# State-space layer of a decoder: residual sum moved from VectorE and GpSimd to TensorE and ScalarE

## The chip, the core and the metric

The kernel runs on one core of one Trainium2 chip. The metric is the device time of one execution in microseconds. The engines are TensorE (PE, with its weight loads as PEld), VectorE (DVE), ScalarE (ACT), GpSimd (POOL) and SyncE (SP, which issues the DMAs). Each engine takes its own instructions in the order in which the program lists them. They meet only at semaphores: an instruction waits until a counter has reached a value, and a finished instruction raises a counter.

## The reference, cut to what matters

The network is a decoder of two layers over x of 64 sequences, 128 tokens and 128 channels, all in float32. The fourth of its six steps is the state-space layer:

```python
x = _layernorm(x + _L1_attn_ref(x, W_in, b_in, conv_w, conv_b, x_proj_w, dt_proj_w,
                                dt_bias, A_log, D_param, W_out, b_out))
# in _L1_attn_ref, E = 256 channels, N = 16 states:
z = x @ W_in + b_in
xc, xr = z[..., :E], silu(z[..., E:])
xc = silu(causal_conv(xc, 4 taps) + conv_b)
dt, Bm, Cm = split(xc @ x_proj_w)
delta = softplus(dt @ dt_proj_w + dt_bias)
h_t = exp(delta * A) * h_(t-1) + delta * xc * B_t      # 16 states per channel
y_t = sum over states of h_t * C_t
return ((y + xc * D_param) * xr) @ W_out + b_out
```

The x that goes in is itself the layer norm of the sum before it. So the layer has to form: normalised x, plus the output product, plus the output bias.

## The kernel before, in words

The layer is `phase_scan`. It handles the 64 sequences in 16 groups of four, so a tile holds 128 partitions by 512 columns (by 1024 where both halves of the 256 channels are in one tile). Every group g has a body on each engine, and every body loops over the 16 states n. What an engine does at a state is written out by hand, so the order of the work is the order of these loops and nothing else. Work for the groups g+1, g+2 and g+3 and the leftovers of group g-1 are slotted between the states.

A state goes round the engines in this way.

- POOL multiplies `du` by B (`drive_state`, line 1872) into one of three `drive` buffers.
- ACT computes the decay, one instruction for each half (`decay_state`, line 2025). There is one `decay` tile in PSUM, so each half waits until DVE has scanned the same half of the state before.
- DVE runs two scans, one for each half (`scan_state`, line 2239), and then, for 13 of the 16 states, multiplies the state by C (`read_state`, line 2252). For the states 3, 7 and 13 ("aside") POOL does that product (line 1882).
- PE adds the product to `y_ps` with the identity as stationary operand (`sum_state`, line 2387; `sum_aside`, line 2395).

Around these, PE also makes 156 "lots" for the next phase (`make_lot`, line 2314, into one of the two banks `f0_ps` and `f1_ps`). ACT copies each lot out (`take_lot`, line 2066) and SP stores it.

These are the places that the change touches:

- `normalise` on ACT (line 1932), in the slot of state 13 for group g+3: it writes normalised x of a group into the tile `xs`, with four instructions.
- `turn` on PE (line 2324), at state 0 for group g+2: it transposes `xs`. ACT copies the result to `xT` at state 2 (`copy_xT`, line 1943).
- `add_bo` on POOL (line 1819), at state 3 for group g+2 and twice ahead of the loop: x = `xs` + output bias.
- `gate_y` on DVE (line 2261), after state 0, for group g-1: it ends that group's y and raises `y_ready`.
- `project_out` on PE (line 2410), at state 1 and after `sum_state(1)` and the lot of that slot, for group g-1: eight products of 128 by 128 into the bank `f1_ps`; then it raises `o_ready`.
- `leave_group` on DVE (line 2268), after state 3, for group g-1: x = `f1_ps` + x; then it raises `x_steps`.

After the loop, group 15 goes through `gate_y`, `project_out` and `leave_group` once more, with nothing beside them. Ahead of the loop stands a prologue in which DVE adds the residual of the phase before to x (`combine`, line 2167) and finds the statistics. The root of the last batch of statistics on ACT (line 1922) stands ahead of the first decay.

In ACT's body the slot of state 2 is this, and the decay of state 3 comes behind it:

```python
for n in range(states):
    decay_state(g, s, n)
    for unit in taken_at(g, n, n + 1):
        take_lot(unit)
    ...
    if n == 2 and ahead(g, 2):
        copy_xT(g + 2, s)
```

Of the kernel before, what the change touches and what calls it, by code (L numbers as in the profile page):

```python
# [10 lines left out]
ALU = mybir.AluOpType  # L11
# [1507 lines left out]
def phase_scan(core):  # L1519
# [24 lines left out]
    with ExitStack() as ctx:  # L1544
# [15 lines left out]
        early = sb("s_early", [128, halves, taps - 1])  # L1560
        skip_w = sb("s_skip_w", [128, halves, 128])
        shift = sb("s_shift", [128, B])
        xs = sb("s_xs", [128, GB, 128])
        xT = sb("s_xT", [128, GB, taps - 1 + T])
        conv = sb("s_conv", [128, halves, GB, T])
        conv_sig = sb("s_conv_sig", [128, halves, GT])
# [41 lines left out]
        rates = sig("s_rates")  # L1608
        prepared = sig("s_prepared", 6)
        x_normed = sig("s_x_normed")  # L1610
        bo_added = sig("s_bo_added")
        x_turned = sig("s_x_turned")
        xT_ready = sig("s_xT_ready")
        z_ready = sig("s_z_ready", 4)
# [187 lines left out]
        def _(pool):  # L1802
# [11 lines left out]
            nc.gpsimd.memset(xT[:, :, 0:taps - 1], 0.0).then_inc(cleared.sem, 1)  # L1814
            nc.gpsimd.memset(dtT[:, :], 1.0).then_inc(cleared.sem, 1)

            def add_bo(g, s):
                pool.wait_ge(x_normed.sem, x_normed.at(g, 1))
                nc.gpsimd.tensor_tensor(x[:, ds(g * GB, GB), :], xs[:, :, :],
                                        core.w["s_bo"][:, :].unsqueeze(1).broadcast_to([128, GB, 128]),  # L1820
                                        ALU.add).then_inc(bo_added.sem, 1)

            def fix_conv(g, s):

                pool.wait_ge(z_copied.sem, z_copied.at(g, halves))
# [61 lines left out]
            def body(g, s):  # L1887
                for n in range(states):
                    drive_state(g, s, n)
                    if n - 2 in aside:  # L1890
                        read_aside(g, n - 2)
                    if n == 1 and ahead(g, 1):
                        gate_u(g + 1, 1 - s)
                    if n == 3 and ahead(g, 2):
                        add_bo(g + 2, s)
                    if n == 7 and ahead(g, 1):
                        gate_res(g + 1, 1 - s)
                    if n == 12 and ahead(g, 1):
                        make_delta(g + 1, 1 - s)
                    if n == 13 and ahead(g, 1):  # L1900
                        mult_du(g + 1, 1 - s)
                    if n == 14 and ahead(g, 2):
                        fix_conv(g + 2, s)

            add_bo(0, 0)
            fix_conv(0, 0)
            gate_u(0, 0)
            add_bo(1, 1)
            gate_res(0, 0)
            make_delta(0, 0)  # L1910
            mult_du(0, 0)
# [4 lines left out]
        def _(act):  # L1916
# [7 lines left out]
            def normalise(g, s):  # L1924
                for n, batch in enumerate(batches):
                    if g in batch:
                        act.wait_ge(folded.sem, folded.at(n, 9))
                if behind(g, 1):
                    act.wait_ge(bo_added.sem, bo_added.at(g - 1, 1))
                    act.wait_ge(x_turned.sem, x_turned.at(g - 1, 1))  # L1930
                for j in range(GB):
                    last = nc.scalar.activation(xs[:, j, :], x[:, g * GB + j, :], ACT.Identity,
                                                bias=shift[:, ds(g * GB + j, 1)],
                                                scale=core.rstd[:, ds(g * GB + j, 1)])
                last.then_inc(x_normed.sem, 1)
# [93 lines left out]
            def body(g, s):  # L2029
# [4 lines that stand above are left out]
                    if n == 5 and ahead(g, 1):  # L2034
                        tanh_res(g + 1, 1 - s)
                        open_res(g + 1, 1 - s)
                    if n == 2 and ahead(g, 2):
                        copy_xT(g + 2, s)
                    if n == 4 and ahead(g, 1):
                        copy_proj(g + 1, 1 - s)  # L2040
                    if n == 6 and ahead(g, 1):
                        take_raw(g + 1, 1 - s)
                    if n == 8 and ahead(g, 1):
                        soft_exp(g + 1, 1 - s)
                    if n == 10 and ahead(g, 1):
                        soft_ln(g + 1, 1 - s)
                    if n == 11 and ahead(g, 2):
                        copy_conv(g + 2, s, 0)
                    if n == 12 and ahead(g, 2):
                        copy_conv(g + 2, s, 1)  # L2050
                    if n == 13 and ahead(g, 3):
                        normalise(g + 3, 1 - s)
                    if n == 14 and ahead(g, 2):
                        copy_res(g + 2, s, 0)
                        copy_res(g + 2, s, 1)
                    if n == 15 and ahead(g, 2):
                        tanh_conv(g + 2, s)
                        open_conv(g + 2, s)

            def take_lot(unit):  # L2060
                j, n = unit // parts, unit % parts
# [68 lines left out]
            around(act, body)  # L2130
            for unit in taken_at(NG, 0, states):
                take_lot(unit)

        @block.vector
        def _(dve):
# [125 lines left out]
                nc.vector.tensor_tensor(res_gate[:, s, :, :], y_ps[:, :, :], res_gate[:, s, :, :],  # L2261
                                        ALU.mult).then_inc(y_ready.sem, 1)

            def leave_group(g, s):
                dve.wait_ge(o_ready.sem, o_ready.at(g, 1))
                dve.wait_ge(bo_added.sem, bo_added.at(g, 1))
                here = x[:, ds(g * GB, GB), :].rearrange("p b d -> p (b d)")
                nc.vector.tensor_tensor(here, f1_ps, here, ALU.add).then_inc(x_steps.sem, 1)

            def body(g, s):  # L2270
                for n in range(states):
                    scan_state(g, s, n)
                    if n not in aside:
                        read_state(g, s, n)
                    if n == 0 and behind(g, 1):
                        gate_y(g - 1, 1 - s)
                    if n == 3 and behind(g, 1):
                        leave_group(g - 1, 1 - s)

            around(dve, body)  # L2280
            gate_y(NG - 1, 1)
            leave_group(NG - 1, 1)

        @block.tensor
        def _(pe):
# [32 lines left out]
            def turn(g, s):  # L2318
# [2 lines left out]
                if behind(g, 1):  # L2321
                    pe.wait_ge(z_copied.sem, z_copied.at(g - 1, 3))
                for j in range(GB):
                    last = nc.tensor.transpose(f0_ps[:, j * 128:(j + 1) * 128], xs[:, j, :], core.ident[:, :])
                last.then_inc(x_turned.sem, 1)

            def project_conv(g, s, m):
# [69 lines left out]
                last.then_inc(aside_summed.sem, 1)  # L2397

            def project_out(g, s):
                pe.wait_ge(y_ready.sem, y_ready.at(g, 1))  # L2400
                if ahead(g, 2):
                    pe.wait_ge(z_copied.sem, z_copied.at(g + 2, 4))
                elif ahead(g, 1):
                    pe.wait_ge(raw_taken.sem, raw_taken.at(g + 1, 2))
                else:
                    pe.wait_ge(x_steps.sem, x_steps.at(g - 1, 1))
                lot_gone(g + 1, 1, 1)
                for j in range(GB):
                    for m in range(halves):
                        last = nc.tensor.matmul(f1_ps[:, j * 128:(j + 1) * 128], res_gate[:, s, m, j * 128:(j + 1) * 128],  # L2410
                                                core.w["s_w_out"][:, m, :], start=(m == 0), stop=(m == halves - 1))
                last.then_inc(o_ready.sem, 1)

            def body(g, s):
# [1096 lines left out]
```

## Time and profile before

| what | us |
| --- | --- |
| median of 3 runs | 2777.88 (2777.25 to 2780.86) |
| the profiled execution's own time | 2776.81 |
| its span, first to last instruction | 2774.9 |
| first scan of the state-space layer | 1095.9 |
| last `leave_group` of the layer | 2045.5 |

The profile is that of one execution. Between its span and its own time lie 1.9 us. In the timelines a row is: start, length, engine, line of the kernel, operation, written tile <- read tiles, shape, and how many instructions of the same kind were merged; in square brackets stands how long the engine was idle just before, and what ended that.
### The profile page before, as it was taken

The page shows a single profiled execution, that of the slowest core. Times are in us where ns is not written, and L with a number is a line of the kernel's source. Part 1 is how long each engine was busy: PE and PEld are TensorE (multiplying, and loading weights), DVE is VectorE, ACT ScalarE, POOL GpSimd, SP SyncE. Part 2 cuts the span into 40 slices and gives each one's busy share as a digit, 9 for nine tenths or more (in the row PEclk, how much of TensorE's full clock was granted, in tenths as well). Part 3 has the DMA queues.
Part 4 walks back from the last instruction along what each step waited for, and adds up shares of the span by engine and source line. Part 5 has one row for each costly group of instructions (what it writes and reads, how often), then busy time and mean ns, then how long its engine had stood idle before and what let it go on. Part 6 is the DMA issues. An engine that isn't in the chain of part 4 may idle for free. (4 is left out here: it accounts for less than half of the span.)

```text
span 2774.9 us, 42509 instructions
## 1 busy us (share of the span) xinstructions
PE 2466.6 (89%) x13058; PEld 1468.1 (53%) x13058; DVE 2235.6 (81%) x3698; ACT 1722.6 (62%) x3447; POOL 2000.4 (72%) x1817
## 2 busy tenths in 40 slices
PE   7969999989979976989898899898989999999675
PEld 5646666656646652333333333343348888877232
DVE  5879999856634449999999999999867777777898
ACT  7847777743312226667766776766655665554897
POOL 5539999847746664999999999999836666666244
PEclk9979999999989988999999999999999999999556
DMA  5921111001135535445454554544633323332000
GB/s 164 422 76 22 24 23 22 10 27 44 41 109 162 155 111 192 175 185 188 176 199 161 198 184 171 193 176 176 218 123 84 87 86 87 88 87 74 12 24 28
DMA packets 238434, 331.94 MB, mean 120 GB/s; under 512 B 46433, under 2 KB 186998, under 8 KB 217346
## 3 DMA queue, kind: packets, MB, share of 16 engines
q1 hardware_dynamic: 227538, 311.48, 33.8%
q0 software_dynamic: 9088, 16.94, 1.7%
q8 instruction: 109, 1.79, 0.3%
q14 instruction: 115, 0.94, 0.1%
q10 hardware_dynamic: 1584, 0.79, 0.1%
HBM read 231.45 MB, written 99.50 MB: 119 GB/s over the span
## 5 line engine op out<-in xcount | busy, mean ns | idle before, releaser
L1872 POOL TENSOR_TENSOR s_drive<-s_du,s_b_sb 128x1024 f32<-128x1024 f32 x256 | 600.3, 2359 | 40.1 <-DVE s_state_ps L2239 39.9
L2239 DVE TENSOR_TENSOR_SCAN s_state_ps<-s_decay_ps,s_drive 128x512 f32<-128x512 f32 x416 | 487.1, 1216 | 44.3 <-ACT s_decay_ps L2025 35.4
L2387 PE MATMUL s_y_ps<-s_read,w_ident 128*128 128x512 f32 x832 | 407.3, 616 | 89.0 <-DVE s_read L2252 88.8
L2025 ACT ACTIVATE s_decay_ps<-s_delta,neg_rate 128x508 f32<-128x508 f32 x512 | 340.8, 682 | 151.1 <-DVE s_state_ps L2239 93.4
L2387 PEld LDWEIGHTS s_y_ps<-s_read,w_ident 128*128 128x128 f32 x832 | 149.8, 192 | 323.0 <-DVE s_read L2252 182.9
L2252 DVE TENSOR_TENSOR s_read<-s_state_ps,s_c_sb 128x1024 f32<-128x1024 f32 x208 | 254.6, 1224 | 7.2
L1418 POOL DMA_INDIRECT m_y_scratch<-e_y,e_index x156 | 152.6, 978 | 91.1 <-DVE e_y L1464 49.3
L2686 POOL TENSOR_TENSOR c_share<-c_p,c_norm 128x1232 f32<-128x1232 f32 x64 | 148.2, 2315 | 83.0 <-DVE c_norm L2821 83.0
L743 ACT ACTIVATE b_pT<-b_turn_ps 77x512 f32<-77x512 f32 x256 | 144.3, 591 | 74.6 <-PE b_turn_ps L875 74.6
L2922 PE MATMUL c_f_ps<-c_ctxT,w_c_wqk 128*128 128x308 f32 x512 | 179.4, 438 | 6.2 <-DMA c_ctxT<-in_ctxT_dram 3.6
L1046 POOL DMA_INDIRECT m_rows_scratch<-m_xs,m_index x128 | 128.3, 1003 | 60.1 <-issue 39.9
L677 POOL TENSOR_TENSOR b_p<-b_p,b_top 128x1232 f32<-128x1232 f32 x64 | 143.9, 2248 | 35.8 <-DVE b_top L805 35.8
L2314 PE MATMUL s_f_ps<-w_c_wvo,s_lotT 128*128 128x512 f32 (+1 forms) x312 | 154.0, 600 | 14.2 <-ACT s_res L1959 10.3
L2066 ACT ACTIVATE s_stage<-s_f_ps 128x512 f32<-128x512 f32 (+1 forms) x156 | 89.9, 588 | 118.0 <-PE s_f_ps L2314 111.4
L2965 PEld LDWEIGHTS c_turn_ps<-c_vp,c_pT 128*128 128x128 f32 (+1 forms) x1280 | 152.4, 192 | 14.1 <-issue 6.2
L2735 ACT ACTIVATE c_k<-c_f_ps,key_bias 128x308 f32<-128x308 f32 x256 | 132.6, 518 | 43.1 <-PE c_f_ps L2922 42.4
L2965 PE MATMUL c_turn_ps<-c_vp,c_pT 128*128 128x128 f32 (+1 forms) x1280 | 153.7, 275 | 4.6 <-ACT c_pT L2760 4.6
L875 PE MATMUL b_turn_ps<-w_ident,b_p 128*77 128x128 f32 x1024 | 152.6, 282 | 0.0
L2755 ACT ACTIVATE c_pT<-c_turn_ps 128x512 f32<-128x512 f32 x128 | 69.7, 595 | 131.9 <-PE c_turn_ps L2956 131.9
L2818 DVE TENSOR_REDUCE c_norm<-c_p 128x16 f32<-128x1232 f32 x64 | 91.9, 1436 | 69.8 <-ACT c_p L2747 69.8
L683 POOL TENSOR_TENSOR b_p<-b_p,b_norm 128x1232 f32<-128x1232 f32 x64 | 143.9, 2249 | 2.2 <-DVE b_norm L811 2.2
L2940 PE MATMUL c_s_ps<-c_k,c_xT 128*128 128x308 f32 x512 | 143.2, 421 | 0.7 <-DVE c_p L2809 0.7
(376 smaller groups left out, 6153.7 us busy)
## 6 DMA issues: line engine op xcount, KB each, us to landing
s_b_sb<-s_bc_scratch SPq DMA_DIRECT2D x64, 1024.0 KB, 6.2
s_c_sb<-s_bc_scratch SPq DMA_DIRECT2D x64, 1024.0 KB, 5.4
c_vp_scratch<-s_stage SPq DMA_DIRECT2D x152, 256.0 KB, 2.6
c_vp<-c_vp_scratch SPq DMA_DIRECT2D x64, 576.0 KB, 4.2
m_rows_scratch<-fill SPq DMA_DIRECT2D x33, 1040.0 KB, 27.0
e_w<-in_m_we_dram SPq DMA_DIRECT2D x39, 384.0 KB, 3.2
e_xg<-m_rows_scratch SPq DMA_DIRECT2D x39, 260.0 KB, 3.4
s_read<-m_y_scratch SPq DMA_DIRECT2D x32, 256.0 KB, 3.1
```

The costliest lines, as they stand in the source:

```text
L743: nc.scalar.activation(pT[:, j, :, :], turn_ps[0:S2, j % 2, :].rearrange("p (r t) -> p r t", t=128), ACT.Copy).then_inc(pT_ready.sem, 1)
L875: last = nc.tensor.transpose(turn_ps[0:S2, j % 2, r * 128:(r + 1) * 128], p[:, s, per * r + j, :], core.ident[:, :])
L1418: nc.gpsimd.indirect_dma_start(y_dram[:, :], bass.IndirectOffsetOnAxis(index[:, t % y_slots, j:j + 1], 0), y[:, t % y_slots, j, :], None, ...
L1872: nc.gpsimd.tensor_tensor(drive[:, (g * states + n) % drives, :, :], du[:, s, :, :], b_sb[:, n, :].unsqueeze(1).broadcast_to([128, halves, ...
L2025: nc.scalar.activation(decay[:, m, :, 1:], delta[:, s, m, :].rearrange("p (b t) -> p b t", t=T)[:, :, 1:], ACT.Exp, scale=core.neg_rate[:, ...
L2239: nc.vector.tensor_tensor_scan(home[:, h, :], decay[:, h, :, :].rearrange("p b t -> p (b t)"), drive[:, (g * states + n) % drives, h, :], ...
L2252: nc.vector.tensor_tensor(read[:, r % deep, :, :], state[:, :, :], c_sb[:, n // per_chunk % 2, n % per_chunk, :].unsqueeze(1).broadcast_to ...
L2314: nc.tensor.matmul(f_ps[0:lot_width(j), bank, :], lotT[:, j % lot_slots, 0:lot_width(j)], wvo[:, 4 * part:4 * part + 4, :].rearrange("p h ...
L2387: last = nc.tensor.matmul(y_ps[:, m, :], core.ident[:, :], read[:, r % deep, m, :], start=False, stop=False)
L2686: nc.gpsimd.tensor_tensor(share[:, i % 2, :].rearrange("p (s h) -> p h s", h=heads), p[:, i % p_slots, :, :], norm[:, i % 2, :].unsqueeze( ...
L2922: nc.tensor.matmul(f_ps[:, mine % 2, 0:GB * S2], core.w["c_wqk"][:, h, :], ctxT[:, g % 2, :], start=True, stop=True).then_inc(front_ready. ...
L2965: last = nc.tensor.matmul(y_ps, pT[0:width(c), i % 2, c, :], vp[0:width(c), i % vp_slots, c, :], start=(c == 0), stop=(c == lumps - 1))
```

## The change

- `xs` goes away. ACT's `normalise` writes normalised x over x, in place, and no longer waits for `add_bo` and `turn` of the group before. `turn` reads x.
- `add_bo` on POOL goes away.
- `project_out` on PE gets two products of 512 columns ahead of its eight: the identity times x of the group, and the identity times the bias, repeated for the four sequences. All ten accumulate in `f1_ps`. The wait for `y_ready` now stands behind these two.
- `leave_group` leaves DVE. ACT gets it as a copy of `f1_ps` to x, behind `copy_xT` in the slot of state 2, and behind its last lots for group 15.

```diff
-            def add_bo(g, s):
-                pool.wait_ge(x_normed.sem, x_normed.at(g, 1))
-                nc.gpsimd.tensor_tensor(x[:, ds(g * GB, GB), :], xs[:, :, :],
-                                        core.w["s_bo"][:, :].unsqueeze(1).broadcast_to([128, GB, 128]),
-                                        ALU.add).then_inc(bo_added.sem, 1)
...
-                    if n == 3 and ahead(g, 2):
-                        add_bo(g + 2, s)
...
-            add_bo(0, 0)
             fix_conv(0, 0)
             gate_u(0, 0)
-            add_bo(1, 1)
             gate_res(0, 0)
...
-                if behind(g, 1):
-                    act.wait_ge(bo_added.sem, bo_added.at(g - 1, 1))
-                    act.wait_ge(x_turned.sem, x_turned.at(g - 1, 1))
                 for j in range(GB):
-                    last = nc.scalar.activation(xs[:, j, :], x[:, g * GB + j, :], ACT.Identity,
+                    last = nc.scalar.activation(x[:, g * GB + j, :], x[:, g * GB + j, :], ACT.Identity,
...
                     if n == 2 and ahead(g, 2):
                         copy_xT(g + 2, s)
+                    if n == 2 and behind(g, 1):
+                        leave_group(g - 1)
...
+            def leave_group(g):
+                act.wait_ge(o_ready.sem, o_ready.at(g, 1))
+                nc.scalar.activation(x[:, g * GB:(g + 1) * GB, :].rearrange("p b d -> p (b d)"), f1_ps,
+                                     ACT.Copy).then_inc(x_steps.sem, 1)
...
             for unit in taken_at(NG, 0, states):
                 take_lot(unit)
+            leave_group(NG - 1)
...
-            def leave_group(g, s):
-                dve.wait_ge(o_ready.sem, o_ready.at(g, 1))
-                dve.wait_ge(bo_added.sem, bo_added.at(g, 1))
-                here = x[:, ds(g * GB, GB), :].rearrange("p b d -> p (b d)")
-                nc.vector.tensor_tensor(here, f1_ps, here, ALU.add).then_inc(x_steps.sem, 1)
...
-                    if n == 3 and behind(g, 1):
-                        leave_group(g - 1, 1 - s)
...
-                    last = nc.tensor.transpose(f0_ps[:, j * 128:(j + 1) * 128], xs[:, j, :], core.ident[:, :])
+                    last = nc.tensor.transpose(f0_ps[:, j * 128:(j + 1) * 128], x[:, g * GB + j, :], core.ident[:, :])
...
             def project_out(g, s):
-                pe.wait_ge(y_ready.sem, y_ready.at(g, 1))
...
                 lot_gone(g + 1, 1, 1)
+                pe.wait_ge(x_normed.sem, x_normed.at(g, 1))
+                nc.tensor.matmul(f1_ps, core.ident[:, :], x[:, g * GB:(g + 1) * GB, :].rearrange("p b d -> p (b d)"),
+                                 start=True, stop=False)
+                nc.tensor.matmul(f1_ps.rearrange("p (b d) -> p b d", b=GB), core.ident[:, :],
+                                 core.w["s_bo"][:, :].unsqueeze(1).broadcast_to([128, GB, 128]),
+                                 start=False, stop=False)
+                pe.wait_ge(y_ready.sem, y_ready.at(g, 1))
                 for j in range(GB):
                     for m in range(halves):
                         last = nc.tensor.matmul(f1_ps[:, j * 128:(j + 1) * 128], res_gate[:, s, m, j * 128:(j + 1) * 128],
-                                                core.w["s_w_out"][:, m, :], start=(m == 0), stop=(m == halves - 1))
+                                                core.w["s_w_out"][:, m, :], start=False,
+                                                stop=(j == GB - 1 and m == halves - 1))
                 last.then_inc(o_ready.sem, 1)
```

## Rows read from the trace of the kernel before

**Rows 1.** Windows: one group of the loop, scan to scan
```profile
core 0: us, PE busy (x) PEld busy (x) DVE busy (x) ACT busy (x) POOL busy (x), PEclk, DMA share, GB/s
1500.20:1558.90 58.70, 52.75 (x134) 22.32 (x132) 54.75 (x48) 41.00 (x62) 54.92 (x26) 1.00 0.48 180
```
**Rows 2.** Line 2239 (DVE's scans): its engine sat idle until (us, times)
```profile
  ACT s_decay_ps L2025: 48.6, 75
```
**Rows 3.** Timeline of DVE in that group
```profile
1514.87 1.22 DVE L2252 TENSOR_TENSOR s_read<-s_state_ps,s_c_sb 128x1024 f32<-128x1024 f32 x1
...
1519.70 2.33 DVE L2239 TENSOR_TENSOR_SCAN s_state_aside<-s_decay_ps,s_drive 128x512 f32<-128x512 f32 x2
1521.95 0.66 DVE L2268 TENSOR_TENSOR x<-s_f_ps,x 128x512 f32<-128x512 f32 x1
1522.53 2.33 DVE L2239 TENSOR_TENSOR_SCAN s_state_ps<-s_decay_ps,s_drive 128x512 f32<-128x512 f32 x2
...
1526.27 2.35 DVE L2239 TENSOR_TENSOR_SCAN s_state_ps<-s_decay_ps,s_drive 128x512 f32<-128x512 f32 x2 [0.15 <-ACT s_decay_ps L2025]
...
1540.47 2.35 DVE L2239 TENSOR_TENSOR_SCAN s_state_ps<-s_decay_ps,s_drive 128x512 f32<-128x512 f32 x2 [1.16 <-ACT s_decay_ps L2025]
```
**Rows 4.** Timeline of ACT in that group
```profile
1515.49 0.58 ACT L1943 ACTIVATE s_xT<-s_f_ps 128x512 f32<-128x512 f32 x1
1517.44 0.69 ACT L2025 ACTIVATE s_decay_ps<-s_delta,neg_rate 128x508 f32<-128x508 f32 x1 [1.38 <-DVE s_state_ps L2239]
...
1524.38 0.59 ACT L1992 ACTIVATE s_bc_rows<-s_f_ps 32x512 f32<-32x512 f32 x1 [1.62 <-PE s_f_ps L2355]
...
1538.22 0.60 ACT L2066 ACTIVATE s_stage<-s_f_ps 128x512 f32<-128x512 f32 x1 [1.69 <-PE s_f_ps L2314]
```
**Rows 5.** Timeline of PE and its weight loads in that group
```profile
1516.14 0.30 PEld L2387 LDWEIGHTS s_y_ps<-s_read,w_ident 128*128 128x128 f32 x2 [0.64 <-DVE s_read L2252]
...
1517.97 1.02 PE L2314 MATMUL s_f_ps<-w_c_wvo,s_lotT 128*128 128x512 f32 x2
1518.82 1.95 PE L2410 MATMUL s_f_ps<-w_s_w_out,s_res_gate 128*128 128x128 f32 x16
...
1526.18 1.98 PE L2387 MATMUL s_y_ps<-s_read,w_ident 128*128 128x512 f32 x4 [1.84 <-DVE s_read L2252]
```
**Rows 6.** Lines 2268 and 1819: lengths in ns (min/median/max), first and last start
```profile
L2268 DVE TENSOR_TENSOR x<-s_f_ps,x x16: 662/663/691, 1169.9 to 2045.5; 128x512 f32<-128x512 f32 x16
...
L1819 POOL TENSOR_TENSOR x<-s_xs,w_s_bo x16: 1279/1292/1735, 1044.9 to 1865.8; 128x512 f32<-128x512 f32 x16
```
**Rows 7.** Timeline of PE and DVE in group 14
```profile
1928.21 1.95 PE L2410 MATMUL s_f_ps<-w_s_w_out,s_res_gate 128*128 128x128 f32 x16
...
1929.95 2.33 DVE L2239 TENSOR_TENSOR_SCAN s_state_aside<-s_decay_ps,s_drive 128x512 f32<-128x512 f32 x2
...
1936.43 3.54 PE L2387 MATMUL s_y_ps<-s_read,w_ident 128*128 128x512 f32 x4 [2.51 <-DVE s_read L2252]
...
1944.66 2.34 DVE L2239 TENSOR_TENSOR_SCAN s_state_aside<-s_decay_ps,s_drive 128x512 f32<-128x512 f32 x2 [0.89 <-ACT s_decay_ps L2025]
```
**Rows 8.** Windows: the stretch of group 14 behind PE's pause
```profile
1936.40:1939.90 3.50, 3.47 (x5) 0.98 (x5) 3.40 (x3) 3.16 (x4) 3.50 (x3) 0.54 0.71 281
```
**Rows 9.** Timeline of PE and DVE in group 15 and at the layer's end
```profile
1992.42 1.95 PE L2410 MATMUL s_f_ps<-w_s_w_out,s_res_gate 128*128 128x128 f32 x16
...
1992.44 2.33 DVE L2239 TENSOR_TENSOR_SCAN s_state_aside<-s_decay_ps,s_drive 128x512 f32<-128x512 f32 x2
...
2043.44 2.02 PE L2410 MATMUL s_f_ps<-w_s_w_out,s_res_gate 128*128 128x128 f32 x16 [0.77 <-ACT s_stage L2066]
```
**Rows 10.** Timeline of the prologue, DVE and ACT
```profile
1057.08 1.47 DVE L2167 TENSOR_TENSOR x<-x,s_read 128x512 f32<-128x512 f32 x2
...
1059.37 4.36 DVE L2167 TENSOR_TENSOR x<-x,s_read 128x512 f32<-128x512 f32 x2
...
1093.56 0.25 ACT L1922 ACTIVATE stat_root<-rstd 128x52 f32<-128x52 f32 x1 [5.18 <-DVE rstd L2188]
```

More of the change, by code:

```diff
@@ L1562, in phase_scan @@
         shift = sb("s_shift", [128, B])
-        xs = sb("s_xs", [128, GB, 128])
         xT = sb("s_xT", [128, GB, taps - 1 + T])
@@ L1610, in phase_scan @@
         x_normed = sig("s_x_normed")
-        bo_added = sig("s_bo_added")
         x_turned = sig("s_x_turned")
@@ L2276, in body @@
                         gate_y(g - 1, 1 - s)
-                    if n == 3 and behind(g, 1):
-                        leave_group(g - 1, 1 - s)
             around(dve, body)
             gate_y(NG - 1, 1)
-            leave_group(NG - 1, 1)
         @block.tensor
```

## The prediction

> **What bounds the kernel now.** The change touches only the state-space layer, so I read that layer's rows and take the rest of the kernel as it is. The first view is a window over one group of its loop. In 58.70 us DVE is busy for 54.75, POOL for 54.92, PE for 52.75 and ACT for 41.00 [rows 1]. Three engines are nearly full, so the shares alone don't say which of them sets the pace. The second view does: what ended the idle time ahead of DVE's scans. In the whole layer it was ACT's decay, 75 times, 48.6 us in sum [rows 2], 3.0 us for each of 16 groups, and no other engine is named there. So DVE sets the pace, and where it pauses it waits for ACT. POOL and PE are full, but they follow.
>
> The third view is the timeline around the slot that changes. It shows how ACT, which is busy for only 41 of 58.7 us, comes to hold up DVE: at 1538.22 ACT starts the copy of a lot for which it had waited 1.69 us on PE, and DVE's scan at 1540.47 then starts 1.16 us late, because the decay stood behind that copy in ACT's queue [rows 3, 4]. A wait of ACT for PE is therefore a cost that reaches DVE. The change adds such a wait.
>
> **What is removed.** DVE's `leave_group` has 16 instructions of 663 ns [rows 6]. In the loop each costs DVE less than its length, since neighbours overlap a little: from its start at 1521.95 to the next scan at 1522.53 is 0.58 us [rows 3]. That is what one group gains on the engine that sets the pace. POOL's `add_bo` has 16 instructions of 1292 ns at the median [rows 6]; 14 are in the loop, where no scan was late through POOL [rows 2], so I take nothing for them. The two waits taken from `normalise` were for work of the group before, done more than a state's time ahead: nothing. `normalise` in place has the same four instructions, and `turn` the same four transposes.
>
> **What is added on PE.** Two products of 512 columns with the identity. The nearest row is a lot, one product of 512 columns: from 1517.97 to the next instruction at 1518.82 is 0.85 us [rows 5]. Two are 1.70 us for each group. From below I bound the pair by 0.85 us, if the repeated bias row should cost nothing; from above by 3.54 us, the length of two such products in the slowest row [rows 7]. I take 1.70, since these have the shape of the ordinary row. PE has room for that: 52.75 of 58.70 us. What counts is where they stand.
>
> **What is added on ACT, and the wait.** ACT's copy of `f1_ps` to x has the form of `copy_xT`, 0.58 us [rows 4]. Ahead of it ACT waits for `o_ready`. Behind it in ACT's queue stand the two decays of state 3, a lot, the decays of state 4 and the copies for `project_dt`; DVE waits for the decays, and POOL and PE wait for DVE. So I follow the chain in one ordinary group:
>
> - DVE's product of state 1 ends at 1514.87 + 1.22 = 1516.09 [rows 3]; PE, which waited for it, starts `sum_state(1)` at 1516.14, the lot at 1517.97 and `project_out` at 1518.82 [rows 5].
> - With 1.70 us of new products ahead, the eight old ones start at 1520.52, and, 1.95 us long [rows 5], end at 1522.47. That `y_ready` is asked for later doesn't help: in DVE's order `gate_y` stands ahead of the product of state 1, so it is over by then.
> - ACT is through with `copy_xT` at 1515.49 + 0.58 = 1516.07 [rows 4] and then waits 6.4 us. Its copy ends at 1523.05, the first decay of state 3, 0.69 us long [rows 4], at 1523.74.
> - DVE's scan of state 3 started at 1519.70 [rows 3]. It now starts at 1523.74, **4.04 us later**.
> - Less the 0.58 us of `leave_group`, 3.46 us remain. One old pause goes: ACT waited 1.62 us for PE at 1524.38, which made the scan at 1526.27 late by 0.15 us [rows 3, 4]; PE's products for it come only 1.70 us later while ACT and DVE come 3.5 us later, so ACT finds them done. That leaves **3.3 us for each group**. `x_steps`, for which `project_dt` waits, is raised at 1523.05, ahead of PE's sum at 1526.18 in front of it. The next to be late is again what was late before, the scan at 1540.47.
>
> PE's own pause ahead of `sum_state(4)` grows from 1.84 us [rows 5] by 3.46 - 1.70 to 3.6 us. In group 14 a pause of 2.51 us was followed by the same products in 3.54 instead of 1.98 us, at a granted clock of 0.54, near the 1.2 GHz level, and DVE's scan of state 7 was then 0.89 us late for ACT [rows 5, 7, 8]. I expect this drop in most groups and take nothing for it: the 0.89 us lie ahead of the 1.16 us that DVE waits two states later [rows 3] for a lot whose place hangs on the product of state 6, which isn't delayed, so the second pause shrinks by what the first costs.
>
> **The sum.** The loop has 13 ordinary groups with a `leave_group` (1 to 13): 13 x 3.3 = 43.0 us. Group 14 has no lot ahead of `project_out`: 1928.21 + 1.70 + 1.95 + 0.58 + 0.69 = 1933.13 against the scan at 1929.95 [rows 7], so 3.2 - 0.6 = 2.6 us. In group 15 PE is behind with its lots: 1992.42 + 4.92 = 1997.34 against 1992.44 [rows 9], so 4.9 - 0.6 = 4.3 us. At the layer's end PE reaches `project_out` at 2043.44 only after ACT's last lot [rows 9], so the new products lie open: 1.70 + 0.58 - 0.66 = 1.6 us.
>
> The prologue gives something back. Two of DVE's additions took 4.36 us where 1.47 is usual, while POOL's multiplication and the second `add_bo` ran, and ACT waits for DVE until the root at 1093.56, just ahead of the first decay [rows 10]. Between nothing and the whole length of the two `add_bo` there, 1.3 + 1.7 = 3.0 us [rows 6], I take the middle, 1.5 us, since only part of the 2.9 us can be due to `add_bo`. The Trainium skill, SBUF — State Buffer, section "SBUF: two separate sides", says that a VectorE instruction with two SBUF inputs and a GpSimd instruction that reads SBUF exclude each other for the whole instruction. By it the sum would have the 3.0 us here; the trace agrees in kind, for 4.36 us stand against 1.47 only beside POOL's work.
>
> 43.0 + 2.6 + 4.3 + 1.6 - 1.5 = **50.0 us**. On the profiled execution's own time of 2776.81 us (span 2774.9 and 1.9 around it) that is 2826.8; the median of the runs shown is 1.1 us higher, and gives 2827.9, so **2828 us**.
>
> **The rivals.**
>
> *The wait is covered and DVE gains (faster).* This is ACT's slot of state 2: if `o_ready` came before ACT needs to start the decay of state 3 at 1517.44 [rows 4], less the copy, so by 1516.9, DVE would keep its schedule and only lose `leave_group`. Price: 15 x 0.58 + 1.5 = 10.2 us, 2768 us. For it speaks that DVE is the engine that sets the pace and gets lighter. Against it, `project_out` doesn't even start before 1518.82 [rows 5], with the old work alone. Chance 0.05.
>
> *The new products cost PE nothing visible (smaller loss).* The chain is then 1.70 us shorter: 3.3 - 1.7 = 1.6 us for 13 groups, 0.9 and 2.6 for the last two, 23 us after the prologue, 2801 us. For it: PE has pauses, 0.64 us just before `sum_state(1)` [rows 5]. Against it: the products are listed behind that sum and the lot, and PE runs those without a pause. Chance 0.06.
>
> *The clock stays low for longer (larger loss).* If the half rate lasts beyond `sum_state(4)` into `project_dt`, which ACT also waits for, that is another 1.6 us, of the size seen on the sum (3.54 - 1.98), or more. Of 0.89 + 1.9 us the pause of 1.16 us takes up a part, 1.6 us remain, 13 x 1.6 = 21 us: 2849 us. For it: a pause of 3.6 us is longer than any in an ordinary group. Against it: in group 14 the clock was back after that one stretch. Chance 0.16. The Trainium skill, TensorE: Matmul & The Clock Gate, Part 1, says that the array runs at half rate after it has been idle and returns to full rate under work. By that rule alone this rival's time would hold in every group; the one pause of 2.51 us in the trace agrees on the fall, and the return came within a stretch.
>
> **How the numbers follow.** The forecast has 0.73, the three rivals 0.05, 0.06 and 0.16. The lower bound of the pair of products takes 0.85 x 15 = 13 us and the prologue another 1.5: 2813. The upper bound is 1.84 us for each of 15 groups, 28 us: 2856, with the third rival below it at 2849. I give 2812 to 2850, which leaves out the first two rivals and the upper end of the third. A change of 0.2% is 5.6 us, about what a measurement of this kernel can tell from none. Faster by more: 0.05, the first rival. Within it: 0.02, for mixtures of the first two. Slower: 0.93.
>
> **What would show it.** In the changed kernel's timeline ACT's copy at state 2 should be preceded by an idle time of some 6 us that ends with `project_out`; the scan of state 3 should start about 4 us late for ACT's decay, in every group; a group should last near 62 us instead of 58.7; DVE's waits for ACT should rise from 48.6 to some 100 us. PE's granted clock should fall behind a pause near 3.6 us once in a group. The prediction is wrong if that wait is below 3 us, if ACT's copy finds `o_ready` raised, or if POOL or PE takes ACT's place as what ends the waits of the scans.

## The result and the profile after

The changed kernel takes 2859.26 us (median of 4 runs, 2852.02 to 2870.04), beside 2779.37 us for the kernel before (4 runs, 2777.25 to 2781.47). The ratio is 1.0291, with an interval of 1.0255 to 1.0327. So it is slower, as forecast, but by 80 us where 50 were forecast, and above the top of the range. The profiled execution took 2862.4 us, with a span of 2860.6.

The first reading is the one that the prediction named, the idle time ahead of DVE's scans in the changed kernel (us, times), beside [rows 2]:

```profile
  ACT s_decay_ps L2010: 128.1, 85
  POOL s_drive L1864: 1.8, 2
```

ACT's decay is still what DVE waits for, and nothing took its place. (The two waits with POOL's name are ACT's too: the `drive` that the scan reads was done 4.7 us earlier, the decay 0.13 us before the scan.) But the sum rose by 79.5 us, not by the 50 or so that were expected. That is about the size of the whole loss. The second reading is windows over two groups, over the same stretch in each, and over a stretch of a third (columns as in [rows 1]):

```profile
1290.00:1354.90 64.90, 59.16 (x137) 24.70 (x136) 54.34 (x46) 41.40 (x62) 53.66 (x25) 0.92 0.46 165
1545.40:1607.50 62.10, 54.45 (x137) 23.09 (x136) 54.23 (x46) 41.41 (x62) 53.60 (x25) 1.00 0.46 172
...
1308.30:1318.50 10.20, 10.12 (x13) 3.49 (x13) 7.98 (x8) 5.99 (x8) 10.20 (x5) 0.55 0.78 312
1563.70:1573.90 10.20, 8.57 (x19) 3.35 (x20) 9.96 (x9) 7.20 (x10) 10.20 (x5) 1.00 0.76 303
...
1439.00:1442.40 3.40, 3.40 (x5) 1.10 (x4) 3.28 (x4) 2.26 (x3) 3.40 (x3) 0.50 0.76 294
```

There are three kinds of group. The short ones (6, 7 and 12) are 62.2 us long at a full clock, as forecast. The long ones last some 64.9 us, and in them the granted clock is near the lower level, 1.2 GHz, for 10.2 us: PE gets through 13 instructions in that stretch instead of 19, although it is busy nearly all of the time. In the groups 5 and 11, of 63.1 us, the clock is at that level for 3.4 us only (the last row is from group 5). So it fell in nine of the groups 1 to 12. From one `gate_y` to the next the groups last:

| groups | before, us | after, us |
|---|---|---|
| 1 to 12 | 58.68 each | 64.93 64.93 64.93 65.13 63.15 62.16 62.16 64.94 64.93 65.04 63.14 62.17 |
| 13 | 58.18 | 61.65 |
| 14 | 62.49 | 69.28 |
| 15 | 57.66 | 64.61 |

DVE's timeline shows where the time goes in a group. The first three rows are from a long group, the last three from a short one: the scans of the states 3, 7 and 9.

```profile
1302.49 2.34 DVE L2232 TENSOR_TENSOR_SCAN s_state_aside<-s_decay_ps,s_drive 128x512 f32<-128x512 f32 x2 [4.05 <-ACT s_decay_ps L2010]
...
1317.68 2.34 DVE L2232 TENSOR_TENSOR_SCAN s_state_aside<-s_decay_ps,s_drive 128x512 f32<-128x512 f32 x2 [1.97 <-ACT s_decay_ps L2010]
...
1325.76 2.35 DVE L2232 TENSOR_TENSOR_SCAN s_state_ps<-s_decay_ps,s_drive 128x512 f32<-128x512 f32 x2 [2.25 <-ACT s_decay_ps L2010]
...
1557.86 2.34 DVE L2232 TENSOR_TENSOR_SCAN s_state_aside<-s_decay_ps,s_drive 128x512 f32<-128x512 f32 x2 [4.05 <-ACT s_decay_ps L2010]
...
1571.00 2.33 DVE L2232 TENSOR_TENSOR_SCAN s_state_aside<-s_decay_ps,s_drive 128x512 f32<-128x512 f32 x2
...
1577.98 2.35 DVE L2232 TENSOR_TENSOR_SCAN s_state_ps<-s_decay_ps,s_drive 128x512 f32<-128x512 f32 x2 [1.16 <-ACT s_decay_ps L2010]
```

Scan 3 waits 4.05 us in both, where the prediction has 4.04. Scan 9 of the short group waits 1.16 us as before [rows 3]. The long group has 1.97 us more at scan 7 and 1.09 us more at scan 9. These make 3.06 us, of which 64.93 - 62.17 = 2.76 are left at the end of the group. ACT's timeline has the same two groups in the same order, the copy of `leave_group`, the first of `take_raw` (state 6) and the lot behind the decay of state 8:

```profile
1301.18 0.60 ACT L2049 ACTIVATE x<-s_f_ps 128x512 f32<-128x512 f32 x1 [6.46 <-PE s_f_ps L2400]
...
1315.03 1.02 ACT L1988 ACTIVATE s_conv_sig<-s_f_ps 128x1024 f32<-128x1024 f32 x1 [3.56 <-PE s_f_ps L2352]
...
1323.51 0.60 ACT L2058 ACTIVATE s_stage<-s_f_ps 128x512 f32<-128x512 f32 x1 [2.77 <-PE s_f_ps L2298]
...
1556.55 0.60 ACT L2049 ACTIVATE x<-s_f_ps 128x512 f32<-128x512 f32 x1 [6.45 <-PE s_f_ps L2400]
...
1567.68 1.03 ACT L1988 ACTIVATE s_conv_sig<-s_f_ps 128x1024 f32<-128x1024 f32 x1 [0.83 <-PE s_f_ps L2352]
...
1575.73 0.60 ACT L2058 ACTIVATE s_stage<-s_f_ps 128x512 f32<-128x512 f32 x1 [1.69 <-PE s_f_ps L2298]
```

`project_bc` and `project_dt` are PE's products for the next group, at the states 2 and 4, which ACT copies out. `leave_group` waits 6.46 us for `project_out`, where 6.4 were forecast. Then, in the long group alone, ACT waits 2.73 us longer for `project_dt` (3.56 against 0.83), and 1.08 us longer for the lot. Both are PE's. PE's timeline shows why; the last two rows are from the short group:

```profile
1296.62 1.02 PE L2298 MATMUL s_f_ps<-w_c_wvo,s_lotT 128*128 128x512 f32 x2
1297.48 1.02 PE L2392 MATMUL s_f_ps<-x,w_ident 128*128 128x512 f32 x2
1298.34 1.02 PE L2394 MATMUL s_f_ps<-w_s_bo,w_ident 128*128 128x512 f32 x2
1299.20 1.95 PE L2400 MATMUL s_f_ps<-w_s_w_out,s_res_gate 128*128 128x128 f32 x16
...
1303.53 1.92 PE L2339 MATMUL s_f_ps<-s_u,w_s_x_proj 128*48 128x512 f32 x4 [0.67 <-ACT s_stage L2058]
...
1308.38 2.92 PE L2371 MATMUL s_y_ps<-s_read,w_ident 128*128 128x512 f32 x4 [2.93 <-DVE s_read L2245]
1311.22 3.77 PE L2352 MATMUL s_f_ps<-s_dtT,w_s_dt_proj 17*128 17x512 f32 x4
1314.93 5.97 PE L2371 MATMUL s_y_ps<-s_read,w_ident 128*128 128x512 f32 x8
...
1563.75 1.98 PE L2371 MATMUL s_y_ps<-s_read,w_ident 128*128 128x512 f32 x4 [2.92 <-DVE s_read L2245]
1565.66 1.98 PE L2352 MATMUL s_f_ps<-s_dtT,w_s_dt_proj 17*128 17x512 f32 x4
```

The chain of the forecast is there, each identity product 0.86 us. Behind PE's pause ahead of `sum_state(4)` the long group runs at about half rate: `sum_state(4)` takes 2.92 us against 1.98 and `project_dt` 3.77 against 1.98, and `sum_state(5)` and `sum_state(6)` are still slow (5.97 us for the pair). The pause was the same in both groups, 2.93 and 2.92 us.

**Where the 85.6 us between the two profiled executions are.** Groups 1 to 12: +63.5, of which 12 x (62.17 - 58.68) = 41.9 are the chain and 21.6 the groups in which the clock fell. Group 13: +3.5. Group 14: +6.8. Group 15: +6.95. The layer's end: +1.6. Group 0: -2.8. The prologue: -0.3. The phases ahead of the layer and behind it: +4.0 and +2.5; the change doesn't touch these.

### The profile page after: what moved, and what is told of

It is laid out like the page before. It is cut to its first block and busy times, and to the rows that moved or that the text cites. A ratio compares the mean times of both kernels' runs of the same rounds, so it can differ in the third digit from the quotient of the medians.

```text
span 2860.6 us, 42577 instructions
## 1 busy us (share of the span) xinstructions
PE 2533.8 (89%) x13110; PEld 1495.6 (52%) x13122; DVE 2227.7 (78%) x3682; ACT 1729.7 (60%) x3463; POOL 1979.3 (69%) x1801
## 3 DMA queue, kind: packets, MB, share of 16 engines
q8 instruction: 109, 1.79, 0.3%
## 5 line engine op out<-in xcount | busy, mean ns | idle before, releaser
L2371 PE MATMUL s_y_ps<-s_read,w_ident 128*128 128x512 f32 x832 | 432.5, 650 | 89.9 <-DVE s_read L2245 89.8
L2371 PEld LDWEIGHTS s_y_ps<-s_read,w_ident 128*128 128x128 f32 x832 | 158.9, 203 | 336.7 <-DVE s_read L2245 169.7
L1874 POOL TENSOR_TENSOR s_state_aside<-s_state_aside,s_c_sb 128x1024 f32<-128x1024 f32 x48 | 112.8, 2350 | 102.3 <-DVE s_state_aside L2232 102.2
L2232 DVE TENSOR_TENSOR_SCAN s_state_aside<-s_decay_ps,s_drive 128x512 f32<-128x512 f32 x96 | 112.1, 1209 | 90.9 <-ACT s_decay_ps L2010 89.1
L2726 ACT ACTIVATE c_k<-c_f_ps,key_bias 128x308 f32<-128x308 f32 x256 | 132.6, 518 | 41.9 <-PE c_f_ps L2913 41.9
```

Source lines behind the costliest of these rows:

```text
L2232: nc.vector.tensor_tensor_scan(home[:, h, :], decay[:, h, :, :].rearrange("p b t -> p (b t)"), drive[:, (g * states + n) % drives, h, :], ...
L2371: last = nc.tensor.matmul(y_ps[:, m, :], core.ident[:, :], read[:, r % deep, m, :], start=False, stop=False)
```

## The experiments

Theory A is the account above: the chain through ACT's new wait costs 3.5 us a group, and the granted clock behind PE's pause costs the rest. Its rivals are a loss by the two products alone and the third rival of the prediction (a low clock that costs 1.6 us in every group).

**e1_filled.** Three products with a tile of zeros fill PE's pause ahead of `sum_state(4)`; they add nothing to `y_ps`.

```diff
                     if n == 2 and ahead(g, 1):
                         project_bc(g + 1, 1 - s)
...
+                        for _ in range(3):
+                            nc.tensor.matmul(y_ps[:, 0, :], zeros[:, :], core.w["s_w_in"][:, 0:512],
+                                             start=False, stop=False)
```

> The changed kernel with three more products of 512 columns on TensorE in each group, right behind project_bc, where TensorE otherwise pauses for 2.9 us. They multiply with zeros and add nothing to y. Theory (the loss beyond the forecast is the clock that falls behind that pause): the pause is filled, the granted clock stays at the full level, every ordinary group lasts about 62.2 us as the undisturbed ones of the changed kernel did, none 64.9, and the time is 2825 to 2838 us with a smaller spread than 2852 to 2870. Rival (TensorE simply has too much work): 2.6 us more of work for each of 15 groups make no group shorter, so 2859 us or more.

Measured: 2831.47 us (4 runs, 2829.4 to 2832.8), 1.0191 of before (1.0175 to 1.0208). A window over one group, PE's timeline at the pause, and what DVE's scans waited for in the whole layer:

```profile
1531.10:1593.30 62.20, 57.32 (x143) 24.17 (x142) 54.29 (x47) 41.42 (x63) 53.69 (x25) 1.00 0.48 172
```

```profile
1299.74 2.84 PE L2429 MATMUL s_y_ps<-w_s_w_in,s_zeros 128*128 128x512 f32 x6
1302.73 1.98 PE L2374 MATMUL s_y_ps<-s_read,w_ident 128*128 128x512 f32 x4 [0.15 <-DVE s_read L2248]
```

```profile
  ACT s_decay_ps L2013: 104.7, 76
```

With 0.15 us of the pause left, the clock stays up in the groups 1 to 14, groups 1 to 12 are all short (62.16 to 62.37 us), `sum_state(4)` takes its 1.98 us, and 2859.3 - 2831.5 = 27.8 us are gone. DVE's waits for ACT are 104.7 us, near the 100 that were forecast. PE was given more work and the kernel became faster. Group 14 fell from 69.28 to 62.99 us, so most of its loss was the clock as well. What is left, 54 us over before, is nearly all the chain.

**e2_leave_at_4.** ACT's copy goes two states down, ahead of the copies that wait for `project_bc`.

```diff
-                    if n == 2 and behind(g, 1):
+                    if n == 4 and behind(g, 1):
                         leave_group(g - 1)
```

> The changed kernel with only ScalarE's leave_group moved, from behind copy_xT at state 2 to just ahead of copy_proj at state 4. Theory (the cost is the wait in front of the decay of state 3): the scan of state 3 is no longer late, the wait ahead of the copy falls from 6.4 to under 1 us, and what is left is copy_proj, which waits for TensorE's 1.7 us of new products and makes the scan of state 5 late by some 2 us, 1.6 us a group net: 2798 to 2808 us, groups of 60 to 60.5 us. Rival (the products or the copy themselves cost the time, wherever the copy stands): still above 2845 us.

Measured: 2812.39 us (4 runs), 1.0121 of before (1.0105 to 1.0137). On ACT, and on DVE:

```profile
1358.29 0.58 ACT L2049 ACTIVATE x<-s_f_ps 128x512 f32<-128x512 f32 x1
...
1361.69 0.59 ACT L1977 ACTIVATE s_bc_rows<-s_f_ps 32x512 f32<-32x512 f32 x1 [2.82 <-PE s_f_ps L2339]
```

```profile
1355.30 2.33 DVE L2232 TENSOR_TENSOR_SCAN s_state_aside<-s_decay_ps,s_drive 128x512 f32<-128x512 f32 x2
...
1363.59 2.35 DVE L2232 TENSOR_TENSOR_SCAN s_state_ps<-s_decay_ps,s_drive 128x512 f32<-128x512 f32 x2 [2.27 <-ACT s_decay_ps L2010]
```

The copy no longer waits and scan 3 isn't late. But PE is still late with `project_bc`, and ACT's next wait, 2.82 us, now makes scan 5 2.27 us late (2.46 us in nearly all other groups). So the wait moved on, to a smaller price: 60.40 us a group, as expected. The clock fell again, in three of every four groups, as these windows over the stretches in the groups 1 and 2 show:

```profile
1184.60:1191.30 6.70, 6.07 (x7) 2.35 (x8) 6.58 (x7) 4.67 (x8) 6.67 (x4) 0.50 0.71 293
1246.00:1249.30 3.30, 2.86 (x4) 1.18 (x4) 3.18 (x4) 3.27 (x5) 3.30 (x2) 0.50 1.00 410
```

The falls of 3.4 us cost nothing here (60.40 us); that of 6.8 us makes every fourth group 0.8 us longer (61.16 to 61.21 us). That is part of the few us by which the time is above what was expected.

**e3_no_products.** The two identity products are left out; the first of each pair of the eight starts its bank region, as before. So x and the bias are missing from the sum.

```diff
-                nc.tensor.matmul(f1_ps, core.ident[:, :], x[:, g * GB:(g + 1) * GB, :].rearrange("p b d -> p (b d)"),
-                                 start=True, stop=False)
-                nc.tensor.matmul(f1_ps.rearrange("p (b d) -> p b d", b=GB), core.ident[:, :],
-                                 core.w["s_bo"][:, :].unsqueeze(1).broadcast_to([128, GB, 128]),
-                                 start=False, stop=False)
...
```

> The changed kernel without the two products with the identity: normalised x and the output bias are left out of the sum, so x becomes the output product alone. Theory: ScalarE's wait shortens from 6.4 to 4.7 us and an undisturbed group lasts 60.4 us (58.7 + 1.6 + 0.1); TensorE's pause ahead of sum_state(4) stays near 3 us, so groups with a fallen clock, some 2 to 3 us longer, can still be there; 2800 to 2830 us. Rival (the two products are the whole cost): back at 2780 us or below.

Measured: 2820.59 us in one run. DVE's timeline of one group has the scans of the states 3, 7, 9 and 13, and ACT's the copy of the lot ahead of the decay of state 13:

```profile
1294.19 2.34 DVE L2232 TENSOR_TENSOR_SCAN s_state_aside<-s_decay_ps,s_drive 128x512 f32<-128x512 f32 x2 [2.33 <-ACT s_decay_ps L2010]
...
1308.26 2.34 DVE L2232 TENSOR_TENSOR_SCAN s_state_aside<-s_decay_ps,s_drive 128x512 f32<-128x512 f32 x2 [0.84 <-POOL s_drive L1864]
...
1314.32 2.35 DVE L2232 TENSOR_TENSOR_SCAN s_state_ps<-s_decay_ps,s_drive 128x512 f32<-128x512 f32 x2 [0.23 <-ACT s_decay_ps L2010]
...
1330.93 2.34 DVE L2232 TENSOR_TENSOR_SCAN s_state_aside<-s_decay_ps,s_drive 128x512 f32<-128x512 f32 x2 [1.74 <-ACT s_decay_ps L2010]
```

```profile
1329.05 0.60 ACT L2058 ACTIVATE s_stage<-s_f_ps 128x512 f32<-128x512 f32 x1 [4.09 <-PE s_f_ps L2298]
```

Scan 3 is late by 2.33 us, 1.72 less than with the products. The time is in the expected range, but the groups are a miss: all of 1 to 12 are 61.24 to 61.55 us long, none 60.4, and none 2 to 3 us longer. The clock falls behind the pause in every group, here for 3.4 us only. This is the small fall that the prediction thought of, and half of its reasoning holds: scan 7 is 0.84 us late (POOL is named, but its `drive` was done at 1303.58 and ACT's decay at 1308.13), and the wait of scan 9 shrinks from 1.16 to 0.23 us. Yet scan 13 waits 1.74 us, and the next run tells what it waits without a fall.

**e6_no_products_filled.** The same, with the filling of the first run.

```diff
                         project_bc(g + 1, 1 - s)
...
+                        for _ in range(3):
+                            nc.tensor.matmul(y_ps[:, 0, :], zeros[:, :], core.w["s_w_in"][:, 0:512],
+                                             start=False, stop=False)
```

> The changed kernel without its two products with the identity (normalised x and the bias are left out of the sum) and with the three products with zeros behind project_bc, so that the clock should not fall. Theory: the two products cost ScalarE's wait their own length, 1.7 us, and nothing else, so a group lasts 62.2 - 1.75 = 60.4 us, without the 1.0 us that the fallen clock added to the groups of the run without fill (61.4 us); 2800 to 2806 us. Rival (the 61.4 us were the price of the wait alone): 61.4 us again.

Measured: 2809.35 us in one run, 60.44 us a group. The groups are as expected; the whole time is 3 us above the range, while the kernel before, beside it, took 2780.91 us (17 runs), 3.5 us more than beside the first runs. DVE's scans 3, 9 and 13, and ACT's copy of the lot:

```profile
1293.53 2.34 DVE L2235 TENSOR_TENSOR_SCAN s_state_aside<-s_decay_ps,s_drive 128x512 f32<-128x512 f32 x2 [2.33 <-ACT s_decay_ps L2013]
...
1313.65 2.35 DVE L2235 TENSOR_TENSOR_SCAN s_state_ps<-s_decay_ps,s_drive 128x512 f32<-128x512 f32 x2 [1.16 <-ACT s_decay_ps L2013]
...
1329.33 2.34 DVE L2235 TENSOR_TENSOR_SCAN s_state_aside<-s_decay_ps,s_drive 128x512 f32<-128x512 f32 x2 [0.80 <-ACT s_decay_ps L2013]
```

```profile
1327.44 0.60 ACT L2061 ACTIVATE s_stage<-s_f_ps 128x512 f32<-128x512 f32 x1 [3.15 <-PE s_f_ps L2301]
```

Scan 7 has no wait, scan 9 has its 1.16 us again, and scan 13 waits 0.80 instead of 1.74 us. So a fall of 3.4 us costs 0.84 - 0.93 + 0.94 = 0.85 us at these scans, and about 1 us over the group (61.4 - 60.44). The 0.94 us at scan 13 come through ACT's wait for the lot, 4.09 against 3.15 us: PE runs from the sum of state 8, which is late by the delay of scan 7, to this lot without a pause. Without a fall on either side the products cost 62.17 - 60.44 = 1.73 us a group.

**e4_reordered.** All parts of the change stay, but PE does `project_out`, the lot of state 1 and `project_bc` at state 0, ahead of or right behind `sum_state(0)`, and ACT's copy stands behind the decay of state 3.

```diff
                         skip(g, s)
+                        if behind(g, 1):
+                            project_out(g - 1, 1 - s)
+                        if g < NG - 2:
+                            for unit in made_at(g, 1):
+                                make_lot(g, unit)
                     if n not in aside:
                         sum_state(g, s, n)
+                    if n == 0 and ahead(g, 1):
+                        project_bc(g + 1, 1 - s)
...
-                    for unit in made_at(g, n):
-                        make_lot(g, unit)
-                    if n == 1 and behind(g, 1):
-                        project_out(g - 1, 1 - s)
-                    if n == 2 and ahead(g, 1):
-                        project_bc(g + 1, 1 - s)
+                    if n != 1 or g >= NG - 2:
+                        for unit in made_at(g, n):
+                            make_lot(g, unit)
```

```diff
                     decay_state(g, s, n)
+                    if n == 3 and behind(g, 1):
+                        leave_group(g - 1)
...
-                    if n == 2 and behind(g, 1):
-                        leave_group(g - 1)
```

> All parts of the change kept, but in another order: project_out goes to state 0, right behind skip, the lot of state 1 behind it, project_bc behind sum_state(0), and ScalarE's leave_group to state 3, behind the decay and ahead of the lot. Theory: ScalarE finds o_ready raised or waits under 0.3 us, copy_proj finds its product done, TensorE has no pause ahead of sum_state(4), and a group gets shorter than before by VectorE's 0.58 us and the old pause of 0.15 us: 58.0 us, 2766 to 2774 us, faster than before by 0.2 to 0.4%. Rival (TensorE has no room for 1.7 us more in a group): groups of 59 us or more, no faster than before.

Measured: 2771.98 us (10 runs), 0.9976 of before (0.9966 to 0.9987). This beats both kernels, if only by 5.4 us. PE's `project_out` and its sums of the states 1, 2 and 4, and ACT's copies of `leave_group` and behind `project_bc`:

```profile
1281.67 1.95 PE L2400 MATMUL s_f_ps<-w_s_w_out,s_res_gate 128*128 128x128 f32 x16
...
1287.97 5.42 PE L2371 MATMUL s_y_ps<-s_read,w_ident 128*128 128x512 f32 x12
```

```profile
1284.69 0.58 ACT L2049 ACTIVATE x<-s_f_ps 128x512 f32<-128x512 f32 x1
...
1288.19 0.57 ACT L1977 ACTIVATE s_bc_rows<-s_f_ps 32x512 f32<-32x512 f32 x1
```

`project_out` is over at 1283.62, a microsecond before ACT comes to the copy, so neither copy has a wait in front, and PE's pause ahead of `sum_state(4)` is gone. A group lasts 58.03 us.

**e5_before_reordered.** The kernel before with PE's part of that order alone; `leave_group` stays on DVE and `add_bo` on POOL.

```diff
                         skip(g, s)
+                        if behind(g, 1):
+                            project_out(g - 1, 1 - s)
...
-                    if n == 1 and behind(g, 1):
-                        project_out(g - 1, 1 - s)
...
```

> The kernel before, with TensorE's order alone changed as in the reordered kernel (project_out at state 0 behind skip, the lot of state 1 behind it, project_bc behind sum_state(0)); add_bo stays on GpSimd and leave_group on VectorE. Theory (in the reordered kernel the gain comes from VectorE losing leave_group, 0.58 us a group, and only 0.1 us from the order): groups of 58.5 to 58.6 us, 2774 to 2779 us, no difference from before that can be measured. Rival (the order is what gained): groups of 58.0 us, as in the reordered kernel, 2768 to 2773 us.

Measured: median 2776.92 us of 12 runs. Eleven took 2772.53 to 2782.15 us, and one took 7481.24, for which no run here shows a cause; without it the ratio is 0.9988 of before (0.9978 to 0.9998). So the time moved a little, by 0.1%, where no measurable difference was expected, and the times alone can't tell the order's share from that of the parts. The groups can. A group is 58.62 us, from `gate_y` to `gate_y`:

```profile
1277.57 1.23 DVE L2261 TENSOR_TENSOR s_res_gate<-s_y_ps,s_res_gate 128x1024 f32<-128x1024 f32 x1 [0.16 <-PE s_y_ps L2395]
...
1336.19 1.23 DVE L2261 TENSOR_TENSOR s_res_gate<-s_y_ps,s_res_gate 128x1024 f32<-128x1024 f32 x1 [0.15 <-PE s_y_ps L2395]
```

So the order gives 0.06 us of a group and the parts of the change 58.62 - 58.03 = 0.59, as much as `leave_group` takes of DVE (0.58 us by [rows 3]). That is what the change is worth where nothing waits for it.

**after_again** and **before_again.** No edit: the two kernels once more, with a new profile.

> The changed kernel once more, unaltered. Theory: the place where the clock falls differs from run to run, so the groups are again a mixture of 62.2 us and of up to 65 us, in another proportion, and the times spread over 10 us or more around 2859 us, while the filled kernel spread over 3.4 us. Rival (the longer groups belong to fixed places, such as the lots or the DMAs of a group): the same eight groups are long again, and the times agree within 3 us.

> The kernel before once more, unaltered, for a second profile. In the first one the layer began 4 us earlier than in all the others, though the code ahead of the layer is the same. Theory (that is a difference from run to run): the layer begins at some other point between 1036 and 1043 us, with groups of 58.68 us as before, in all 12 ordinary ones. Rival (the changed kernel delays the phases ahead of the layer): 1036.7 us again.

Measured: 2859.21 us (4 runs, 2856.58 to 2862.71), 1.0288 of before (1.0273 to 1.0303), and 2780.44 us. The mixture of groups is there again, partly in other groups: group 5, 63.15 us in the first profile, is a long one here. The runs lie within 6 us, closer than the 10 that were expected. In the second profile of before, the layer's first scan stands at 1099.26 us instead of 1095.94, as in the changed kernel (1099.57), and group 0 is 60.60 us long, as in the changed kernel (60.58). In the second profile of the changed kernel these are 1095.24 and 63.35 us, as in the first one of before. So the +4.0 and the -2.8 us of the account above are differences between executions of one kernel. Group 14 of before is 64.22 us long in its second profile, 62.49 in the first.

## Why the prediction was wrong

**What held.** The direction and the mechanism. ACT waits 6.46 us (forecast 6.4), the decay makes scan 3 late by 4.05 us (4.04) in every ordinary group, and no other engine took ACT's place. A fall of the clock was expected in most groups, and it came in nine of twelve. An undisturbed group is 3.49 us longer (3.3). The two products cost 1.73 us (1.70), and the layer's end 1.6 us (1.6). With the clock held by the filling, the whole kernel takes 2831.5 us, against a forecast of 2828. The first two rivals fell: neither is the wait covered nor are the products free.

**What failed: the price of the clock.** The step is "I expect this drop in most groups and take nothing for it: the 0.89 us lie ahead of the 1.16 us that DVE waits two states later [rows 3] for a lot whose place hangs on the product of state 6, which isn't delayed, so the second pause shrinks by what the first costs." Held against the filled kernel, the term measured 27.8 us, not nothing: 21.6 us in the groups 1 to 12, and most of the rest in group 14 (69.28 against 62.99 us). Two things were wrong in it.

- The drop was taken to be as short as the one of group 14, 3.5 us [rows 8]. In the long groups it lasts 10.2 us and takes in `project_dt`, `sum_state(5)` and most of `sum_state(6)`, all ahead of the lot. DVE's product of state 6 is indeed not delayed, but PE comes to it late. Counted from `leave_group`'s copy, ACT takes that lot 22.33 us on in the long group and 19.18 in the short one. It is 3.15 us late, so the wait at scan 9 grows where it was to shrink.
- Even a short drop at this place isn't swallowed. The runs without the products show it: scan 9 gives back 0.93 us as foreseen, but scan 13 takes 0.94. DVE has its delay back by then, but PE, which runs from the sum of state 8 to the lot ahead of scan 13 without a pause, has not. The changed kernel's own groups 5 and 11 are of this kind: scan 13 waits 1.79 us there, and the groups are 1.0 us longer than the short ones. I followed DVE's pauses for two states beyond the drop and stopped at the first that could take it up.

The third rival had the right place, but its 1.6 us a group was too little: a long group costs 2.76 us, in some groups only. That its 21 us are near the 21.6 us of the groups 1 to 12 is luck: too low a price times too many groups. The prediction had set its price beside the rule of the Trainium skill, TensorE: Matmul & The Clock Gate, Part 1 (half rate after the array was idle, full rate again under work); the runs agree with the fall behind a pause, but not with the fall in every group that the prediction drew from the rule.

**Smaller terms.** PE's pause ahead of `sum_state(4)` became 2.93 us, not 3.6: PE now waits 0.67 us for ACT's copy of a lot ahead of `project_bc`, which I had not seen. The prologue gave back 0.3 us (0.7 in the second profiles) where I took 1.5: `add_bo` beside DVE's additions was not what set its length, for the kernel before in PE's new order, with `add_bo`, has a prologue of 58.88 us, against 58.91 in the changed kernel. Group 14 cost 6.8 us (2.6), and with the pauses filled it is 62.99 us, so most of the loss is the clock. What its chain cost isn't shown, since the kernel before has a fall there too [rows 8]. Group 15 cost 6.95 us (4.3), and 5.5 with the filling; the clock still fell there once (3.4 us), so how the 1.2 us beyond the forecast divide isn't shown.

## What to carry to other kernels

Work that moves to an engine brings its wait along, and on an engine that works in order the wait delays whatever stands behind it (here 6.46 us of ACT made a scan 4.05 us late). Put the consumer behind the point where its producer is done, or move the producer up: here the same parts went from 80 us slower to 5 us faster by order alone. A pause on TensorE can cost something even where the engine has time to spare, since the granted clock may fall behind it (here up to 2.8 us a group), so when a pause grows, price the work behind it at half rate, all the way down to every engine that waits for it, before calling it absorbed.

## What was not expected

- The same pause doesn't decide. Behind 2.93 us the clock fell and behind 2.92 us it stayed, in one execution. In the run with ACT's copy at state 4 it fell in three of four groups, with the same pause of 1.77 or 1.78 us in all four, while the kernel before kept it through 1.84 us in its ordinary groups [rows 5]. Yet the groups aren't drawn at random: that run repeats every four groups, and both profiles of the changed kernel have long groups in a row, then one of 63.15 us, then two without a fall. What decides in which group it falls stays open.
- The length of the low stretch differs as well: 10.2 us in the changed kernel's long groups, 3.4 us in its groups 5 and 11 and in each of the groups 1 to 12 of the run without the two products, behind the same pause of 2.93 us. And the place matters: 3.4 us cost 1.0 us a group there, and nothing in the run with ACT's copy at state 4.
- Work that computes nothing paid: three products with zeros a group, on an engine that was already busy for most of the time, took 27.8 us off the kernel.
